# Sixteen sequences of attention and FFN on one core: float copies of three halves of z on ScalarE, and another order of calls ahead of the loop

## Chip, cores and metric

The kernel runs on one core of one Trainium2 chip. The metric is device time in microseconds of one execution; the time before is the median of three runs.

## What is computed

For 16 sequences of 1024 rows of 256 floats, a transformer block with layer norms without weights, in f32:

```python
qkv = einsum('bnd,ed->bne', layernorm(x), W_qkv) + b_qkv      # Q, K, V of 256 each
attn = softmax(Q @ K.T / sqrt(256)) @ V
x = x + layernorm(attn)
h = silu(layernorm(x) @ wg.T) * (layernorm(x) @ wu.T)          # 768 wide, integer weights / 127
x = x + layernorm(h @ wd.T)
```

## The kernel before

Every f32 operand of a product is split into a high and a low f16 part (names ending in h and l), and each product is made of three f16 matmuls (high by high, high by low, low by high; two where the weights are exact in f16). The scores come from one projection: z is x times a matrix A made of Wq and Wk, plus a bias `cb`, and the scores are z times the transposed x. The exponentials times x come next, and the V projection last.

A sequence b has eight tiles of 128 rows, in two groups g of four. For each half of z (b, g), TensorE's `project_z` (`first_z` for b = 0) leaves two PSUM banks. `z_high` on ScalarE (line 502) makes `zTh`, f16, from them; `z_float` on VectorE (line 732) makes the float copy `zw` from the same banks, once its turn in the list has come; `z_low` on GpSimd or VectorE (line 376) subtracts the two into `zTl`. `zw` is one buffer, so a copy waits for the `z_low` ahead of it. `score` of tile i reads `zTh`, `zTl` and the turned x; the banks of z are free for another product when both `zTh` and `zw` are made. Then come `row_max` (VectorE), `exp` and `p_high` (ScalarE), `p_low` (GpSimd; VectorE for tiles 1 and 4), and two transposes by DMA, `turn_p`, issued by SyncE. `Ph` and `Pl` have three slots, so a later `p_high` waits for transposes. `attend` needs the four tiles of its group. Attention's output goes through `o_high`, `o_low` and `project_v` (VectorE's `y_scale`, `y_stats`, GpSimd's `y_norm`), is added to x and normalized (`x1_add`, `x1_norm`, `y_hat`, `y_high`, `y_low`), and turned by `turn_y`. `gate_up` makes two of twelve products a step, `silu`, `h_mul`, `h_high` and `h_low` follow, then `down`.

Weights are scaled and split at run time: `ffn_max` (VectorE) takes the maximum of one matrix, `powers` and `V_scales`, `ffn_scales` make scales of them, `ffn_high` (ScalarE) and `ffn_low` (VectorE) make the f16 parts, `turn_ffn` turns them by DMA.

All order is written out by hand: each of the five engines has one list of such calls, which it works off strictly in that order, each call waiting on semaphores. SyncE's list holds nearly all DMAs. What comes first (sequence 0, and sequence 1's attention scores) is written out call by call; a loop over b = 1 to 12 takes up the rest, in which the feed-forward part of b, the attention of b and the scores of b + 1 are mixed. The change lies in the part written out ahead of that loop; in the loop `z_float` stays on VectorE.

Of the kernel before, what the change touches and what calls it, by code (L numbers as in the profile page):

```python
# [2263 lines left out]
```

## Time and profile before

| | |
|---|---|
| median of 3 runs | 1363.91 us (1363.36 to 1363.94) |
| the profiled execution | 1363.66 us |
| its span in the profile | 1361.9 us |
| TensorE busy | 1347.7 us, 7414 matmuls |
| VectorE, ScalarE, GpSimd busy | 901.8, 878.1, 832.4 us |
| granted TensorE clock | full in all slices |
| mean DMA rate | 115 GB/s |

A profile tells for each engine when each instruction ran and which other engine's signal it had waited for. A matmul's row is longer than the distance to the next one's start, as matmuls overlap, so the busy share says little about small holes; starts in a row say more. The first 105 us are the stretch that the change rewrites, with the first iteration of the loop beginning at 130.

### The profile page before, as it was taken

The numbers are of one execution on the slowest core, as the hardware profiler recorded it, in microseconds if no ns is written. First come the engines' busy times: TensorE is split into PE (matmuls) and PEld (weight loads), VectorE is DVE, ScalarE is ACT, GpSimd is POOL, SyncE is SP. The second block draws the span as 40 slices with busy tenths as digits, with TensorE's granted clock in tenths as the row PEclk, the third lists the DMA queues.
The fourth block names the chain that finished last, engine by engine and source line by source line (L and its number), as shares of the span: only waits on it lengthen the run. The fifth ranks groups of instructions, "written<-read, shape, count | busy, mean of one in ns | idle before, by whom it ended". The sixth has DMA issues, their size and how long they took to land.

```text
span 1361.9 us, 22402 instructions
## 1 busy us (share of the span) xinstructions
PE 1347.7 (99%) x7414; PEld 725.8 (53%) x7414; DVE 901.8 (66%) x2167; ACT 878.1 (64%) x1378; POOL 832.4 (61%) x1001
## 2 busy tenths in 40 slices
PE   8999999999999999999999999999999999999998
PEld 5445455555555555555554555545555555555555
DVE  7895675666766666666766657667666676656556
ACT  6765775666757577475665766567566675756645
POOL 5686483765847648475584746748376584754635
PEclk9999999999999999999999999999999999999999
DMA  5996482835638366392753827448373563725512
GB/s 180 184 194 138 88 153 79 140 101 115 133 86 157 68 132 140 70 169 65 131 132 71 162 79 127 121 92 147 80 142 100 114 134 86 136 66 100 110 32 64
DMA packets 432968, 157.24 MB, mean 115 GB/s; under 512 B 413905, under 2 KB 416337, under 8 KB 432850
## 3 DMA queue, kind: packets, MB, share of 16 engines
q1 hardware_dynamic: 432048, 154.99, 55.2%
q8 instruction: 61, 1.00, 0.3%
q10 hardware_dynamic: 802, 0.79, 0.2%
q14 instruction: 57, 0.47, 0.1%
HBM read 36.70 MB, written 16.78 MB: 39 GB/s over the span
## 4 chain that ended last, share of the span: by engine, by line
PE 92%; POOL 2%; DVE 2%; DMA 2%; ACT 1%; issue 1%; SPq 0%; DVEq 0%; ACTq 0%; POOLq 0%
PE S L868 91%; DMA yTl<-yl 1%; POOL xl L368 1%; POOL Pl L386 0%; POOL yl L413 0%; DVE st L721 0%; DVE S L768 0%; DMA xs<-in_L_attn_t 0%; DVE mxs L739 0%; POOL xs L356 0%; PE S L897 0%; DVE st L777 0%; ACT yn L531 0%; DMA xTl<-xl 0%; POOL rs L331 0%
## 5 line engine op out<-in xcount | busy, mean ns | idle before, releaser
L511 ACT ACTIVATE P<-S,nmx,sc 128x1024 f32<-128x1024 f32 x128 | 153.6, 1200 | 267.1 <-DVE nmx L743 264.9
L805 DVE SCALAR_TENSOR_TENSOR hf<-S,sc,hf 128x512 f32<-128x512 f32 x192 | 141.9, 746 | 140.8 <-ACT hf L546 135.2
L739 DVE TENSOR_REDUCE mxs<-S 128x1 f32<-128x1024 f32 x128 | 156.1, 1220 | 115.7 <-PE S L868 115.7
L386 POOL TENSOR_TENSOR Pl<-P,Ph 128x1024 f16<-128x1024 f32 x96 | 205.1, 2138 | 30.1 <-issue 26.0
L868 PE MATMUL S<-PTh,xh 128*128 128x512 f16 x512 | 194.1, 379 | 0.0
L868 PE MATMUL S<-PTl,xh 128*128 128x512 f16 x512 | 194.0, 379 | 0.0
L868 PE MATMUL S<-PTh,xl 128*128 128x512 f16 x512 | 194.0, 379 | 0.0
L868 PE MATMUL S<-xTh,zTh 128*128 128x512 f16 x506 | 191.8, 379 | 2.0 <-ACT P L511 1.0
L868 PE MATMUL S<-xTh,zTl 128*128 128x512 f16 x508 | 192.5, 379 | 0.0
L868 PE MATMUL S<-xTl,zTh 128*128 128x512 f16 x508 | 192.5, 379 | 0.0
L327 POOL TENSOR_SCALAR rs<-mv,sc 128x2 f32<-128x2 f32 (+2 forms) x96 | 34.6, 361 | 227.4 <-DVE mv L781 184.9
L422 POOL TENSOR_TENSOR hTl<-hf,hTh 128x512 f16<-128x512 f32 x128 | 146.4, 1158 | 42.4 <-ACT hTh L553 42.4
L868 PE MATMUL S<-Wh,hTh 128*128 128x256 f16 x768 | 170.3, 273 | 0.0
L868 PE MATMUL S<-Wh,hTl 128*128 128x256 f16 x768 | 170.3, 273 | 0.0
L546 ACT ACTIVATE hf<-S,sc 128x512 f32<-128x512 f32 x192 | 130.6, 682 | 52.5 <-POOL hTl L422 37.7
L331 POOL TENSOR_TENSOR rs<-rs,mhalf 128x4 f32<-128x4 f32 (+2 forms) x160 | 145.5, 909 | 13.3
L868 PE MATMUL S<-yTh,Gh 128*128 128x512 f16 x384 | 145.6, 379 | 2.4 <-DMA yTl<-yl 2.4
L868 PE MATMUL S<-yTl,Gh 128*128 128x512 f16 x384 | 145.5, 379 | 0.0
L868 PE MATMUL S<-yTh,Uh 128*128 128x512 f16 x384 | 145.5, 379 | 0.0
L868 PE MATMUL S<-yTl,Uh 128*128 128x512 f16 x384 | 145.5, 379 | 0.0
L553 ACT ACTIVATE hTh<-hf 128x512 f16<-128x512 f32 x192 | 119.5, 624 | 35.4 <-DVE hf L805 35.4
L518 ACT ACTIVATE Ph<-P 128x1024 f16<-128x1024 f32 x128 | 134.8, 1054 | 4.2 <-DMA PTl<-Pl 1.1
(155 smaller groups left out, 2486.0 us busy)
## 6 DMA issues: line engine op xcount, KB each, us to landing
xs<-in_L_attn_t SPq DMA_DIRECT2D x32, 512.0 KB, 5.3
X<-in_L_attn_t SPq DMA_DIRECT2D x32, 512.0 KB, 4.5
out_x<-X SPq DMA_DIRECT2D x62, 256.0 KB, 2.9
PTh<-Ph SPq DMA_TRANSPOSE x128, 3.2
PTl<-Pl SPq DMA_TRANSPOSE x128, 3.2
hTl<-in_L_ffn_w_gate SPq DMA_DIRECT2D x1, 768.0 KB, 6.8
hTh<-in_L_ffn_w_up SPq DMA_DIRECT2D x1, 768.0 KB, 8.8
hTl<-in_L_ffn_w_down SPq DMA_DIRECT2D x1, 768.0 KB, 10.1
```

The costliest lines, as they stand in the source:

```text
L327: p.engine.tensor_scalar(rs, var, scalar1=eps, scalar2=mul, op0=ALU.add, **({} if mul is None else {"op1": ALU.mult})).then_inc(g_step, 1)
L331: return p.engine.tensor_tensor(out=rs, in0=rs, in1=mhalf[:, 0:rs.shape[1]], op=ALU.pow)
L368: p.engine.tensor_tensor(out=xl[k][:, gs, :], in0=src, in1=xh[k][:, gs, :], op=ALU.subtract).then_inc(xl_done if b else xl0_done, 1)
L386: p.engine.tensor_tensor(out=Pl[:, m % 3, :], in0=P[:, m % 2, :], in1=Ph[:, m % 3, :], op=ALU.subtract).then_inc(pl_vector if i in PL_ON_V ...
L422: p.engine.tensor_tensor(out=hTl[g][:, c, :], in0=hf[:, n % 3, :], in1=hTh[g][:, c, :], op=ALU.subtract).then_inc(hl_vector if c in HL_ON_ ...
L511: a.engine.activation(P[:, m % 2, :], ps[:, bank:bank + 2, :].rearrange("p a n -> p (a n)"), ACT.Exp, bias=nmx[:, c:c + 1], scale=sS, accu ...
L518: a.engine.activation(Ph[:, m % 3, :], P[:, m % 2, :], ACT.Copy).then_inc(ph_done, 1)
L546: a.engine.activation(hf[:, n % 3, :], ps[:, bank, :], ACT.Silu, scale=sc2[:, 3:4]).then_inc(silu_done, 1)
L553: a.engine.activation(hTh[g][:, c, :], hf[:, n % 3, :], ACT.Copy).then_inc(hh_done, 1)
L739: v.engine.tensor_reduce(mxs[:, c:c + 1], ps[:, bank:bank + 2, :].rearrange("p a n -> p (a n)"), axis=AX.X, op=ALU.max, negate=True).then_ ...
L805: v.engine.scalar_tensor_tensor(out=hf[:, n % 3, :], in0=ps[:, bank + 1, :], scalar=sc2[:, 4:5], in1=hf[:, n % 3, :], op0=ALU.mult, op1=AL ...
L868: done = t.engine.matmul(out, s, m, start=(start and i == 0), stop=(stop and i == len(terms) - 1))
```

## The change

A second function makes the float copy on ScalarE with the same operands, `z_float_scalar`. It takes the place of `z_float` for the halves (0,1), (1,0) and (1,1), standing in ScalarE's list right behind `z_high` of the half (for (1,1) with one `o_high` between). For (0,0), (2,0), (2,1) and in the loop `z_float` stays. In the same stretch the calls of all five lists are put in another order. TensorE's differs in three places, the others' in many. The diff, cut to what the prediction speaks of; a line of "..." marks what is left out:

```diff
+        def z_float_scalar(a, b, g, bank):
+            a.wait_ge(cb_ready, 1)
+            for dj in range(2):
+                a.wait_ge(z_done, 4 * b + 2 * g + dj + 1)
+                zl_wait(a, b if g else b - 1, 1 - g, dj)
+                a.engine.activation(zw[:, dj, :], ps[:, bank + dj, :], ACT.Identity, bias=cb[:, dj:dj + 1], scale=ZS
+                                    ).then_inc(zw_done, 1)
...
@@ SyncE
             turn_p(s, 0, 4, 0)
+            turn_p(s, 0, 4, 1)
             turn_p(s, 0, 5, 0)
             turn_p(s, 0, 5, 1)
-            turn_p(s, 0, 4, 1)
+            turn_ffn(s, 1, 0)
             turn_p(s, 0, 6, 0)
+            turn_p(s, 0, 6, 1)
             turn_v(s, 0)
             turn_v(s, 1)
-            turn_p(s, 0, 6, 1)
             turn_p(s, 0, 7, 0)
...
             turn_p(s, 1, 1, 0)
-            turn_ffn(s, 1, 0)
             reload(s, 0, 0)
             reload(s, 0, 1)
-            turn_p(s, 1, 1, 1)
+            turn_ffn(s, 2, 0)
+            turn_ffn(s, 2, 1)
             turn_ffn(s, 1, 1)
             turn_p(s, 1, 3, 0)
-            turn_ffn(s, 2, 0)
-            turn_ffn(s, 2, 1)
+            turn_p(s, 1, 3, 1)
+            turn_p(s, 1, 1, 1)
             turn_p(s, 1, 2, 0)
             turn_p(s, 1, 2, 1)
             turn_x(s, 2, 0, 0)
             turn_x(s, 2, 0, 1)
-            turn_p(s, 1, 3, 1)
+            turn_p(s, 1, 4, 0)
             turn_y(s, 0, 0, 0)
-            turn_p(s, 1, 4, 0)
             turn_y(s, 0, 0, 1)
...
@@ GpSimd
+            h_low(p, 0, 1, 1)
+            d_norm(p, 0, 0, 0)
+            z_low(p, 2, 1)
             p_low(p, 1, 6)
             p_low(p, 1, 7)
-            z_low(p, 2, 1)
-            h_low(p, 0, 1, 1)
+            x_norm(p, 3, 0)
             d_norm(p, 0, 0, 1)
...
@@ ScalarE
             z_high(a, 0, 1, 2)
+            z_float_scalar(a, 0, 1, 2)
             x_high(a, 1, 0)
             exp(a, 0, 0, 4)
             p_high(a, 0, 0)
             exp(a, 0, 1, 6)
+            p_high(a, 0, 1)
             exp(a, 0, 2, 0)
-            p_high(a, 0, 1)
+            exp(a, 0, 3, 2)
             p_high(a, 0, 2)
+            p_high(a, 0, 3)
             x_high(a, 1, 1)
-            exp(a, 0, 3, 2)
-            p_high(a, 0, 3)
...
             z_high(a, 1, 0, 2)
+            z_float_scalar(a, 1, 0, 2)
+            exp(a, 0, 6, 0)
+            p_high(a, 0, 6)
             V_high(a)
-            exp(a, 0, 6, 0)
+            ffn_high(a, 0)
             o_high(a, 0, 0, 0)
-            p_high(a, 0, 6)
-            ffn_high(a, 0)
+            exp(a, 0, 7, 4)
             ffn_high(a, 1)
-            exp(a, 0, 7, 4)
+            p_high(a, 0, 7)
             exp(a, 1, 0, 0)
-            p_high(a, 0, 7)
-            z_high(a, 1, 1, 0)
             p_high(a, 1, 0)
             ffn_high(a, 2)
+            z_high(a, 1, 1, 0)
             o_high(a, 0, 0, 1)
+            z_float_scalar(a, 1, 1, 0)
             exp(a, 1, 1, 2)
...
@@ VectorE
             V_max(v)
-            z_float(v, 0, 1, 2)
-            row_max(v, 0, 2, 0)
-            z_low(v, 0, 1)
-            row_max(v, 0, 3, 2)
-            p_low(v, 0, 1)
             ffn_max(v, 0)
             ffn_max(v, 1)
+            z_low(v, 0, 1)
+            p_low(v, 0, 1)
+            row_max(v, 0, 2, 0)
+            row_max(v, 0, 3, 2)
             row_max(v, 0, 4, 4)
+            ffn_max(v, 2)
             row_max(v, 0, 5, 6)
-            ffn_max(v, 2)
             row_max(v, 0, 6, 0)
             p_low(v, 0, 4)
+            powers(v, 1, 5, OB[1], ((1, 2, 2.0 ** -100), (2, 5, 1.0)), 1)
+            row_inverse(v, 0, 0)
+            V_scales(v)
             row_max(v, 0, 7, 4)
-            powers(v, 1, 5, OB[1], ((1, 2, 2.0 ** -100), (2, 5, 1.0)), 1)
-            z_float(v, 1, 0, 2)
-            V_scales(v)
             ffn_scales(v)
...
@@ TensorE
+            gate_up(t, 0, 0, 4, 2, (silu_done, 2), (hmul_done, 2), three)
             project_z(t, 2, 1, 6, (silu_done, 3), (hmul_done, 3))
-            gate_up(t, 0, 0, 4, 2, (silu_done, 2), (hmul_done, 2), three)
...
             gate_up(t, 0, 1, 2, 0, (silu_done, 6), (hmul_done, 6), three)
+            down(t, 0, 0, 0, (x1_done, 6), three)
...
-            down(t, 0, 0, 0, (x1_done, 6), three)
...
+            x_first_turn(t, 1, 0)
             first_z(t, 0, 2, 0)
-            x_first_turn(t, 1, 0)
```

## Rows read from the trace of the kernel before

**Rows 1.** The page's head: busy us (share of the span) xinstructions of each engine.

```profile
PE 1347.7 (99%) x7414; PEld 725.8 (53%) x7414; DVE 901.8 (66%) x2167; ACT 878.1 (64%) x1378; POOL 832.4 (61%) x1001
```

**Rows 2.** Timeline of TensorE: start, us, engine line op out<-in xcount [idle before <-releaser].

```profile
27.20 0.38 PE L868 MATMUL S<-xTh,zTl 128*128 128x512 f16 x1
...
27.89 0.39 PE L868 MATMUL S<-xTh,zTh 128*128 128x512 f16 x1 [0.31 <-DVE zw L732]
...
31.36 0.38 PE L868 MATMUL S<-xTh,zTh 128*128 128x512 f16 x1 [0.70 <-issue]
...
39.56 0.39 PE L868 MATMUL S<-xTh,Ah 128*128 128x512 f16 x1 [0.27 <-DMA xTl<-xl]
...
94.64 0.39 PE L868 MATMUL S<-xTh,zTh 128*128 128x512 f16 x1 [1.02 <-ACT P L511]
...
101.44 0.39 PE L868 MATMUL S<-yTh,Gh 128*128 128x512 f16 x1 [1.45 <-DMA yTl<-yl]
...
364.24 0.39 PE L868 MATMUL S<-yTh,Gh 128*128 128x512 f16 x1 [0.39 <-DMA yTl<-yl]
```

**Rows 3.** Chain that ended last, 88 to 101 us: start us, us, what.

```profile
88.48 0.55 DVE S L768 x2
...
94.77 2.10 POOL yl L413
...
96.89 4.51 DMA yTl<-yl
```

**Rows 4.** Instructions of lines 732 and 502: duration ns min/median/max, first and last start.

```profile
L732 DVE TENSOR_SCALAR zw<-S,cb x64: 720/741/752, 17.0 to 1196.2; 128x512 f32<-128x512 f32 x64
...
L502 ACT ACTIVATE zTh<-S,cb x64: 667/680/703, 16.2 to 1195.3; 128x512 f16<-128x512 f32 x64
```

**Rows 5.** Timeline of VectorE, 17 to 37 us.

```profile
17.05 1.40 DVE L732 TENSOR_SCALAR zw<-S,cb 128x512 f32<-128x512 f32 x2
...
23.73 1.23 DVE L739 TENSOR_REDUCE mxs<-S 128x1 f32<-128x1024 f32 x1 [1.89 <-PE S L868]
...
27.10 1.40 DVE L732 TENSOR_SCALAR zw<-S,cb 128x512 f32<-128x512 f32 x2
...
29.79 1.47 DVE L376 TENSOR_TENSOR zTl<-zw,zTh 128x512 f16<-128x512 f32 x2
...
33.69 1.75 DVE L585 TENSOR_REDUCE am<-hTl 128x1 f32<-128x1536 int32 x1
...
35.35 1.74 DVE L585 TENSOR_REDUCE am<-hTh 128x1 f32<-128x1536 int32 x1
```

**Rows 6.** The page's DMA issues: engine op xcount, KB, us to landing.

```profile
hTh<-in_L_ffn_w_up SPq DMA_DIRECT2D x1, 768.0 KB, 8.8
```

**Rows 7.** SyncE's queue in time; then line 276, 30 to 101 us, and its landings.

```profile
14.84 0.55 SPq L300 DMA_DIRECT2D hTh<-in_L_ffn_w_up  x1
...
40.37 2.70 SPq L276 DMA_TRANSPOSE PTl<-Pl  x2
...
55.53 1.31 SPq L276 DMA_TRANSPOSE PTh<-Ph  x1
...
95.19 1.25 SPq L276 DMA_TRANSPOSE PTh<-Ph  x1
...
L276 SPq DMA_TRANSPOSE PTl<-Pl x13: 1231/1325/2394, 30.1 to 98.2; - x13
...
DMA to landing us min/median/max: 3.1/3.3/6.7
```

**Rows 8.** Timelines of ScalarE and GpSimd, 22 to 60 us.

```profile
22.52 1.05 ACT L495 ACTIVATE xh<-xs 128x1024 f16<-128x1024 f32 x1
...
36.27 4.21 POOL L386 TENSOR_TENSOR Pl<-P,Ph 128x1024 f16<-128x1024 f32 x2
...
55.06 1.56 ACT L470 ACTIVATE X<-hTh,sc 128x1536 f16<-128x1536 int32 x1
...
57.71 1.19 ACT L511 ACTIVATE P<-S,nmx,sc 128x1024 f32<-128x1024 f32 x1
```

More of the change, by code:

```diff
@@ L1094, in _ @@
             turn_p(s, 0, 0, 0)
+            turn_p(s, 0, 1, 0)
             turn_p(s, 0, 0, 1)
-            turn_p(s, 0, 1, 0)
             turn_p(s, 0, 1, 1)
             turn_x(s, 1, 0, 1)
+            turn_p(s, 0, 2, 0)
             turn_p(s, 0, 3, 0)
-            turn_p(s, 0, 2, 0)
             turn_p(s, 0, 2, 1)
@@ L1133, in _ @@
             turn_x(s, 2, 0, 1)
-            turn_p(s, 1, 3, 1)
+            turn_p(s, 1, 4, 0)
             turn_y(s, 0, 0, 0)
-            turn_p(s, 1, 4, 0)
             turn_y(s, 0, 0, 1)
-            turn_p(s, 1, 4, 1)
             turn_x(s, 2, 1, 0)
             turn_x(s, 2, 1, 1)
+            turn_p(s, 1, 4, 1)
             load_x(s, 3, 0)
@@ L1145, in _ @@
             turn_y(s, 0, 1, 1)
+            turn_p(s, 1, 5, 1)
             turn_p(s, 1, 6, 0)
-            turn_p(s, 1, 5, 1)
+            turn_p(s, 1, 6, 1)
             turn_p(s, 1, 7, 0)
-            turn_p(s, 1, 6, 1)
             turn_p(s, 1, 7, 1)
@@ L1277, in _ @@
             x_norm(p, 2, 0)
+            x_norm(p, 2, 1)
             p_low(p, 1, 0)
-            x_norm(p, 2, 1)
+            x_hat_pool(p, 2, 1)
             z_low(p, 1, 1)
-            x_hat_pool(p, 2, 1)
             y_norm(p, 0, 0)
@@ L1298, in _ @@
             h_low(p, 0, 1, 0)
+            h_low(p, 0, 1, 1)
+            d_norm(p, 0, 0, 0)
+            z_low(p, 2, 1)
             p_low(p, 1, 6)
             p_low(p, 1, 7)
-            z_low(p, 2, 1)
-            h_low(p, 0, 1, 1)
+            x_norm(p, 3, 0)
             d_norm(p, 0, 0, 1)
-            d_norm(p, 0, 0, 0)
             h_low(p, 0, 1, 3)
+            x_norm(p, 3, 1)
+            p_low(p, 2, 0)
             h_low(p, 0, 1, 4)
-            x_norm(p, 3, 0)
-            p_low(p, 2, 0)
-            x_norm(p, 3, 1)
             for b in range(1, 13):
@@ L1473, in _ @@
             exp(a, 1, 5, 2)
+            p_high(a, 1, 5)
             exp(a, 1, 6, 0)
-            p_high(a, 1, 5)
             z_high(a, 2, 0, 0)
@@ L1484, in _ @@
             h_high(a, 0, 0, 0)
-            p_high(a, 1, 6)
             h_high(a, 0, 0, 1)
+            silu(a, 0, 0, 3, 0)
             h_high(a, 0, 0, 2)
-            silu(a, 0, 0, 3, 0)
+            silu(a, 0, 0, 4, 2)
             z_high(a, 2, 1, 6)
-            silu(a, 0, 0, 4, 2)
-            silu(a, 0, 0, 5, 0)
             h_high(a, 0, 0, 3)
             h_high(a, 0, 0, 4)
-            p_high(a, 1, 7)
+            silu(a, 0, 0, 5, 0)
             silu(a, 0, 1, 0, 2)
@@ L1500, in _ @@
             h_high(a, 0, 1, 1)
+            p_high(a, 1, 6)
+            p_high(a, 1, 7)
             h_high(a, 0, 1, 2)
@@ L1503, in _ @@
             silu(a, 0, 1, 4, 6)
+            silu(a, 0, 1, 5, 0)
+            x_hat(a, 3, 0)
+            o_high(a, 1, 0, 1)
             h_high(a, 0, 1, 3)
-            silu(a, 0, 1, 5, 0)
-            o_high(a, 1, 0, 1)
             h_high(a, 0, 1, 4)
+            exp(a, 2, 0, 0)
             h_high(a, 0, 1, 5)
-            exp(a, 2, 0, 0)
-            x_hat(a, 3, 0)
-            p_high(a, 2, 0)
             o_high(a, 1, 0, 0)
             exp(a, 2, 1, 2)
+            add_bias(a, 0, 0, 1)
+            p_high(a, 2, 0)
             x_hat(a, 3, 1)
-            add_bias(a, 0, 0, 1)
             add_bias(a, 0, 0, 0)
@@ L1777, in _ @@
             row_max(v, 1, 2, 0)
-            ffn_low(v, 1)
             p_low(v, 1, 1)
             y_scale(v, 0, 0, 0)
+            row_inverse(v, 0, 1)
             y_scale(v, 0, 0, 1)
             y_stats(v, 0, 0, 0)
+            ffn_low(v, 1)
             y_stats(v, 0, 0, 1)
@@ L1787, in _ @@
             x1_add(v, 0, 0, 1)
+            o_low(v, 0, 1, 1)
             o_low(v, 0, 1, 0)
-            o_low(v, 0, 1, 1)
             row_max(v, 1, 4, 0)
@@ L1798, in _ @@
             x1_add(v, 0, 1, 0)
+            row_max(v, 1, 7, 2)
             x1_add(v, 0, 1, 1)
-            row_max(v, 1, 7, 2)
             z_float(v, 2, 0, 0)
@@ L1815, in _ @@
             h_mul(v, 0, 1, 2, 0)
+            x_stats(v, 3, 0)
+            x_stats(v, 3, 1)
+            h_low(v, 0, 1, 2)
             h_mul(v, 0, 1, 3, 2)
[L1817 to L1818 removed]
             h_mul(v, 0, 1, 4, 6)
+            d_stats(v, 0, 0, 0)
+            d_stats(v, 0, 0, 1)
             h_mul(v, 0, 1, 5, 0)
[L1821 to L1823 removed]
             d_add(v, 0, 0, 0)
+            d_add(v, 0, 0, 1)
             row_max(v, 2, 0, 0)
             o_low(v, 1, 0, 1)
[L1827 removed]
             h_low(v, 0, 1, 5)
```

35 lines of the change are left out of this document (13 added, 22 removed).

## The prediction

> **What bounds the kernel now.** I read the head of the page first: TensorE is busy 1347.7 of 1361.9 us [rows 1], so a change of order on other engines can only fill or open holes in TensorE's stream. Then TensorE's instructions in order of time. A 512-column matmul starts every 0.216 us, though its row says 0.38, so the idle time in brackets is some 0.16 short of the real hole: after 27.20 the next start was due at 27.42 and came at 27.89, a hole of 0.47 [rows 2]. Read so, the holes of the stretch in front of the loop are, after the first microseconds: 0.47 ahead of 27.89, 0.86 ahead of 31.36, 0.43 ahead of 39.56, 1.18 ahead of 94.64 and 1.61 ahead of 101.44; behind these the timeline has three more up to the end, of about 0.5 each, of which the first is shown, all in front of `gate_up` in the loop, which the change leaves alone [rows 2]. So 4.5 us stand where the change works.
>
> The last view is the chain of waits from 88.5 to 101.4: `project_v` of (0,1) ends, VectorE scales and sums up y, GpSimd makes `yl` at 94.77, its transpose is issued at 96.89 and lands 4.51 later, and only then `gate_up` starts [rows 3]. From Y to `gate_up` are 12.96 us, in which TensorE has four steps of 2.59: 2.6 us of hole whatever comes ahead. The change keeps the order of `y_scale`, `y_stats`, `y_norm` and `y_low` there. So the holes at 94.64 and 101.44 are one hole in two parts and stay; what can be won is 0.47 + 0.86 + 0.43 = 1.76 us.
>
> **Part by part.** I follow each engine's new list with durations and spacings of before, from 14 us to the loop.
>
> *The three float copies.* One copy of half of z is two instructions; on VectorE one takes 741 ns, the ScalarE instruction of the same shape into f16 takes 680 [rows 4]. Float output on ScalarE isn't in the trace for this shape; between 0.55 and 0.75 (either end is near the rows) I take 0.60, since the next instruction starts a little before one's end. For (0,1) ScalarE is through with `zTh` at 22.5, where it went on with x_high [rows 8], and has both halves at 23.8, in place of VectorE's 27.10 to 28.4 [rows 5]. The bank that `score(0,3)` waits for is free long before 27.4: the hole of 0.47 goes. ScalarE's next step, x_high(1,0), ends at 24.8, still ahead of the exp at 25.2, so its 1.2 us are covered there.
>
> The Trainium skill, page "ScalarE: Activation LUTs", section "Rules for kernel authors", speaks against this part: it gives mul and add to VectorE, which per element is up to about 3 times faster in bf16. The trace has ScalarE the faster by 61 ns on this operand out of PSUM, in f32 [rows 4], so the rule doesn't hold here.
>
> *The low part of that half.* `z_low(0,1)` is what ends the hole at 31.36: VectorE ran it from 29.79 to 31.26 [rows 2, 5]. In the new list it stands behind row_max(0,0), row_max(0,1), V_max, and then **ffn_max(0) and ffn_max(1)**, which came later before. VectorE starts row_max(0,0) at 23.8 (23.73, and 0.1 because both `xTl` now come ahead of the copy that began at 17.05, which idle time of VectorE before 17.05 mostly absorbs [rows 5]). V_max ends 3.37 later (23.73 to 27.10), at 27.2; the two maxima cost 1.66 each by their spacing (33.69 to 35.35), to 30.5; z_low takes up to 1.47, to 31.8 or 32.0 [rows 5]. Their data are there: the load of the second matrix is issued at 14.84 and takes 8.8 [rows 6, 7]. TensorE is ready at 30.1 and starts score(0,4) at 31.98 (with 0.1 of signalling, as 31.26 to 31.36), not 31.36. So: 0.1 for the later first copy, less 0.47, plus 0.99 for a hole of 1.85 instead of 0.86: **+0.62** here. Bounds: -0.6 (one maximum hidden by an earlier start) to +0.9.
>
> *The wait at 39.56.* The `xl` behind it comes from GpSimd at 36.3 and lands by 39.3 to 39.5; TensorE arrives at 39.75: the hole of 0.43 goes, net **+0.19**.
>
> *attend(0,0,0) at 45.8.* Behind z_low, VectorE now has p_low(0,1), then row_max(0,2) (33.0) and row_max(0,3) (to 35.8). exp(0,3) follows at 35.8, p_high(0,2) at 37.0 instead of 32: GpSimd, free at 36.1, waits till 38.1 for its two `Pl` of 4.21 together, which ran from 36.27 [rows 8]: done at 42.4 instead of 40.5. SyncE issues the last of them at 42.4 (before, at the end of 40.37 + 2.70), it lands a median 3.3 later, 45.7, and TensorE needs it at 46.0 [rows 7]. Slack 0.3 where it was 0.8: I take 0, bounds 0 and +0.6.
>
> *project_z(1,1) at 59.7.* It waits for exp(1,0), on ScalarE from 57.71 and done at 59.0 [rows 8]. New: V_scales follows TensorE at 49.7, one row_max is put between it and ffn_scales, so ffn_high(0) starts at 53.1, o_high, exp(0,7), ffn_high(1) and p_high(0,7) come behind, exp(1,0) runs 58.7 to 60.0. TensorE is there at 59.9: **+0.2**, bounds 0 and +0.7. The copy for (1,0) ends at 47.9 and the next exp runs before 49.2, needed at 52.1; the one for (1,1) ends at 65.3, its first half at 64.8, and score(1,2) takes them at 65.3 and 66.6. Both cost nothing while ScalarE keeps that lead of some 0.5 us. project_v(0,0) needs o_low at 67.6 and starts at 67.9; o_low(0,1,1) first now waits for ScalarE at 84.3, ends with its partner at 85.7, and project_v(0,1) starts at 86.1: 0.
>
> *SyncE's queue.* Here the order matters most. turn_ffn(1,0) now stands ahead of turn_p(0,6,0) and both turn_v, and waits for ffn_high(1), 1.57 long, begun at 55.06 before and at 56.3 now [rows 8]: it can't be issued before 57.9. SyncE is through with turn_p(0,5,1) at 55.7, idles 2.2 us, and holds eleven and more transposes behind it. Before, it stood at 55.53 with the same set of transposes (only ordered otherwise) up to yTh, and was free at 96.44, 0.45 ahead of yTl [rows 7]. That is a shift of 2.4; 0.6 was idle time before, 0.45 the lead, 0.35 is given by TensorE's own shift, and an emptied queue takes the next transposes at 1.231 instead of 1.325, shortest and median [rows 7]. Left are 0 to 1.0; turn_ffn(2,1), now ahead of five turns of P, waits for ffn_low(2) at 79.3 to 80.3, just when SyncE gets there. I take yTl issued 0.45 late, **+0.45**, bounds 0 and +2.0 (the whole shift arrives). Its 4.51 to landing against a median 3.3 for the `PTl` [rows 3, 7] may be down to what shared the DMA engines then: that could give back up to 1.2.
>
> *From there to the loop.* down(0,0,0) goes ahead of three gate_up and needs `hTl` of chunk 5 at 18.8 us behind the first gate_up; VectorE has it at 18.75: 0, bounds 0 and +0.7. project_z(2,1) and gate_up(0,0,4) swap at no cost, as chunk 3 is ready earlier. x_norm(3,0), x_hat(3,0) and exp(2,0) end about 2 us later than before, relative to TensorE, which had 3 to spare. The loop then starts from the same waits.
>
> **Sum.** 0.1 - 0.47 + 0.99 - 0.43 + 0.2 + 0.45 = +0.84. The profiled execution took 1363.66 us, 1.8 around its span of 1361.9; the median of the three runs is 1363.91, 0.25 above. 1363.91 + 0.8 = **1364.7**. A measurement can tell about 0.2% from no change, 2.7 us.
>
> **Rivals.** (1) Slower: **the stalled queue reaches yTl in full**. Place: turn_ffn(1,0) at 55.7 to 57.9, and again turn_ffn(2,1) at 80. Price: 2.4 less the lead of 0.45 plus 1 us more for ffn_low(2), on top of the +0.4 ahead of it: about +3.3, 1367.2. It decides once yTl is issued later than 99. For it: SyncE issued almost without a break from 55 to 96; against it: the idle 0.6 and the ring's own slack. Chance 0.13. (2) **The maxima don't delay z_low** (VectorE gets ahead, or their order is hidden): the 1.76 go, and yTl lands as quickly as the `PTl`, 1.2 more: up to -2.9, typically -1.8, 1362.1. For it: the copies do leave VectorE; against it: VectorE has no idle time from 23.73 to 31. Chance 0.10, of which 0.03 beyond 0.2%. (3) **The holes only change place**: all is paid back before 101.44 by the fixed 12.96 and the time is 1363.9. Chance 0.15. (4) **ScalarE is slow on float output.** At three times VectorE's 741 ns an instruction takes 2.2 us [rows 4], 3.2 more for a copy; x_high(1,0) and exp(0,0) come about 2 us late, and with them `Pl` and attend(0,0,0): +3, 1366.9. The f16 row of the same shape, 680 ns, speaks against it: 0.02. The factor of three is that of the Trainium skill's page "ScalarE: Activation LUTs", section "Rules for kernel authors".
>
> **How the numbers follow.** The forecast as worked out, +0.2 to +2.5, has 0.60. Faster by over 0.2%: 0.03. Slower by over 0.2%: 0.13 + 0.02, less what of (1) stays under 2.7 us, 0.12. Same: 0.85. The range runs from rival (2) at 1362.3 to rival (1) at 1367.2.
>
> **What would show it.** Right: no hole ahead of score(0,3); one of about 1.9 us ahead of score(0,4), released by VectorE's zTl at 31.9; none at project_z(1,0); SyncE idle at 56 to 58 ahead of the Uh transpose; yTl issued at 97.5 to 98; gate_up from 102 to 102.5. Wrong: row_max(0,0) much earlier than 23.8, a hole in front of an attend (its `Pl` too late), or any new hole between 102 and 131.

## The result, and the profile after

| | before | after |
|---|---|---|
| median, 16 runs each, taken beside one another | 1364.14 us (1363.09 to 1364.78) | 1366.25 us (1364.75 to 1367.42) |
| profiled execution's span | 1361.9 us | 1364.5 us |
| `gate_up` of sequence 0 starts | 101.44 | 103.92 |

The ratio is 1.0015, 95% interval 1.0009 to 1.0022: 2.1 us slower, where +0.8 was forecast. That is inside the range and under 0.2%, but the interval excludes no change. The added time stands ahead of the loop: 2.48 us by the start of `gate_up`. In the loop the two executions differ by little.

Behind line 502 all line numbers are 9 higher than before (868 is 877, 732 is 741, 739 is 748, 681 is 690); `z_float_scalar` is line 511. The head of the page of after, beside [rows 1]:

```profile
span 1364.5 us, 22400 instructions
...
PE 1348.7 (99%) x7414; PEld 726.1 (53%) x7414; DVE 897.1 (66%) x2161; ACT 881.3 (65%) x1384; POOL 829.4 (61%) x1001
```

Six copy instructions (three halves of two banks) have left VectorE and six have come to ScalarE; TensorE's work is the same. Its timeline, beside [rows 2] (start, us, engine line op out<-in, idle time before and releaser):

```profile
17.23 0.38 PE L985 MATMUL S<-xTh,zTh 128*128 128x512 f16 x1 [0.71 <-ACT zTh L502]
19.45 1.04 PE L959 MATMUL S<-xTh,Ah 128*128 128x512 f16 x4 [0.33 <-DVE zw L741]
...
32.48 0.38 PE L877 MATMUL S<-xTh,zTh 128*128 128x512 f16 x1 [1.63 <-issue]
...
61.52 0.39 PE L877 MATMUL S<-xTh,Ah 128*128 128x512 f16 x1 [0.96 <-ACT P L520]
...
87.78 0.27 PE L877 MATMUL S<-Vh,oTh 128*128 128x256 f16 x1 [0.16 <-issue]
...
96.76 0.39 PE L877 MATMUL S<-xTh,zTh 128*128 128x512 f16 x1 [1.02 <-ACT P L520]
...
103.92 0.39 PE L877 MATMUL S<-yTh,Gh 128*128 128x512 f16 x1 [1.80 <-DMA yTl<-yl]
```

As in the prediction, a hole is the start less the due start. The table holds all of them up to `gate_up`; the measured changes add up to the 2.48 us.

| place | hole before | after | change | in the sum |
|---|---|---|---|---|
| start of `first_z(0)` (17.06, 17.23) | – | – | +0.17 | +0.1, with the next line |
| `first_z(1)`, 19.45 | 0 | 0.49 | +0.49 | |
| `score(0,3)`, 27.89 before | 0.47 | 0 | -0.47 | -0.47 |
| `score(0,4)`, 32.48 | 0.86 | 1.80 | +0.94 | +0.99 |
| wait for `xl`, 39.56 before | 0.43 | 0 | -0.43 | -0.43 |
| `project_z(1,1)`, 61.52 | 0 | 1.12 | +1.12 | +0.2 |
| `project_v(0,1)`, 87.78 | 0 | 0.31 | +0.31 | 0 |
| 96.76 and `gate_up`, 103.92 | 1.18, 1.61 | 1.18, 1.96 | +0.35 | +0.45 |

So two terms hold most of the miss, `first_z(1)` and `project_z(1,1)`. I first show what stands behind each in after.

**`first_z(1)`.** VectorE's timeline of after, beside [rows 5]:

```profile
15.21 1.41 DVE L730 BATCH_NORM_STATS2 st<-xs 128x6 f32<-128x256 f32 x4 [0.34 <-DMA xs<-in_L_attn_t]
...
16.82 1.26 DVE L643 SCALAR_TENSOR_TENSOR xTl<-S,xTh 128x512 f16<-128x512 f32 x2
17.99 1.40 DVE L741 TENSOR_SCALAR zw<-S,cb 128x512 f32<-128x512 f32 x2
...
31.09 1.28 DVE L376 TENSOR_TENSOR zTl<-zw,zTh 128x512 f16<-128x512 f32 x2
```

The copy starts at 17.99 and not 17.05. Of the 0.94, about 0.58 are the second `xTl` (1.26 for two, ahead of the copy; before, 0.69 for one) and 0.36 the statistics, which began at 14.85 before and now wait for a load. SyncE issues the feed-forward weights 2 us sooner (the one of `w_up` at 12.83, [rows 7] has it at 14.84), and they take 11.9 us instead of 8.8 [rows 6]; that their earlier issue is what delays the load of x, I only read from this order.

**`project_z(1,1)`.** It waits for `exp(1,0)`, which waits for `ffn_high(0)`, which waits for the scales that VectorE makes. VectorE, then GpSimd, then ScalarE, of after; the last two lines are VectorE and GpSimd of before:

```profile
50.53 1.90 DVE L690 TENSOR_TENSOR sc<-sc 128x1 f32<-128x1 f32 x1
...
48.05 2.28 POOL L376 TENSOR_TENSOR zTl<-zw,zTh 128x512 f16<-128x512 f32 x2 [3.06 <-ACT zw L511]
50.29 4.21 POOL L386 TENSOR_TENSOR Pl<-P,Ph 128x1024 f16<-128x1024 f32 x2
...
54.63 1.57 ACT L470 ACTIVATE X<-hTl,sc 128x1536 f16<-128x1536 int32 x1 [3.24 <-DVE sc L591]
...
60.18 1.19 ACT L520 ACTIVATE P<-S,nmx,sc 128x1024 f32<-128x1024 f32 x1
...
49.85 0.92 DVE L681 TENSOR_TENSOR sc<-sc 128x1 f32<-128x1 f32 x1
...
48.48 2.28 POOL L376 TENSOR_TENSOR zTl<-zw,zTh 128x512 f16<-128x512 f32 x2 [5.92 <-DVE zw L732]
```

The squaring of one number in each partition takes 1.90 us. It took 0.92 before, and that was no fair price either: it ends at 52.43, GpSimd's first `Pl` at 50.29 + 4.21 / 2 = 52.40; before it ended at 50.77, GpSimd's `zTl` at 50.76. `exp(1,0)` comes at 60.18 where I had 58.7.

**SyncE.** The queue of after, beside [rows 7], then VectorE, then GpSimd:

```profile
54.80 1.34 SPq L276 DMA_TRANSPOSE PTl<-Pl  x1
59.36 1.44 SPq L311 DMA_TRANSPOSE Uh<-X  x1
...
96.73 1.27 SPq L276 DMA_TRANSPOSE PTh<-Ph  x1
98.04 1.32 SPq L282 DMA_TRANSPOSE yTh<-yh  x1
99.41 1.43 SPq L282 DMA_TRANSPOSE yTl<-yl  x1
...
83.10 0.88 DVE L799 SCALAR_TENSOR_TENSOR X<-S,rs,X 128x256 f32<-128x256 f32 x2 [2.12 <-DMA X<-in_L_attn_t]
...
96.85 2.14 POOL L413 TENSOR_TENSOR yl<-yn,yh 128x1024 f16<-128x1024 f32 x1
```

SyncE idles from 56.14 to 59.36 for `turn_ffn(1,0)`. The reload of x that stands behind it comes late, VectorE waits 2.12 us for it at 83.10, and `project_v(0,1)` starts 0.31 late. `yl` is done at 98.99, and its transpose is issued at 99.41, as SyncE is still with `yTh`: the 0.45 of the prediction.

### The profile page after: what moved, and what is told of

Its sections match the earlier page's. It is cut to its first block, busy times and chain, and to the rows that moved or that the text cites. A ratio compares the mean times of both kernels' runs of the same rounds, so it can differ in the third digit from the quotient of the medians.

```text
span 1364.5 us, 22400 instructions
## 1 busy us (share of the span) xinstructions
PE 1348.7 (99%) x7414; PEld 726.1 (53%) x7414; DVE 897.1 (66%) x2161; ACT 881.3 (65%) x1384; POOL 829.4 (61%) x1001
## 4 chain that ended last, share of the span: by engine, by line
PE 87%; SPq 3%; DVE 3%; DMA 2%; issue 2%; ACT 2%; POOL 1%; DVEq 0%; ACTq 0%; POOLq 0%
PE S L877 87%; SPq L276 2%; DMA yTl<-yl 1%; SPq L257 1%; DVE mxs L748 1%; ACT Ph L527 1%; DVE S L777 1%; DVE st L786 0%; POOL Pl L386 0%; DMA PTl<-Pl 0%; SPq L282 0%; DMA xs<-in_L_attn_t 0%; ACT P L520 0%; SPq L246 0%; PE S L906 0%
## 6 DMA issues: line engine op xcount, KB each, us to landing
hTh<-in_L_ffn_w_up SPq DMA_DIRECT2D x1, 768.0 KB, 11.9
```

## The experiments

Every kernel below computes the whole result. Times are medians. Each group of kernels ran on a chip of its own with the kernel before in between (its medians there: 1363.88 to 1364.01, and 1364.14 beside after), and the ratio is to those runs; so medians of different rows compare to some 0.3 us at best. "Start" is the start of `gate_up` in the profile; the median less this start lies between 1261.8 and 1263.4 for all kernels, with 1262.7 before and 1262.3 after, so the start tells what the stretch ahead of the loop does, and under 1 us is lost or won behind it. A start is that of one profiled execution; one kernel that was profiled twice (copies_only) started at 102.85 and at 103.31, so a difference of under 0.5 us between starts is not shown by itself.

| kernel | median us (runs) | ratio, 95% interval | start |
|---|---|---|---|
| before | 1364.14 (16) | 1 | 101.44 |
| after | 1366.25 (16) | 1.0015 (1.0009 to 1.0022) | 103.92 |
| copies_only | 1366.27 (11) | 1.0016 (1.0007 to 1.0025) | 102.85 |
| order_only | 1369.60 (5) | 1.0041 (1.0027 to 1.0055) | 107.61 |
| zlow_first | 1369.62 (5) | 1.0041 (1.0027 to 1.0055) | 106.46 |
| zlow_quiet | 1367.54 (8) | 1.0027 (1.0016 to 1.0037) | 104.62 |
| square_scalar | 1365.03 (11) | 1.0005 (0.9996 to 1.0014) | 102.03 |
| uh_late | 1365.48 (11) | 1.0008 (0.9999 to 1.0017) | 103.64 |
| head_before | 1366.02 (11) | 1.0016 (1.0007 to 1.0025) | 103.29 |
| three | 1364.69 (11) | 1.0006 (0.9997 to 1.0015) | 101.91 |
| all_four | 1368.06 (9) | 1.0026 (1.0016 to 1.0036) | 104.95 |
| three_quiet | 1366.13 (11) | 1.0016 (1.0007 to 1.0025) | 103.39 |
| tuned | 1363.39 (11) | 0.9996 (0.9987 to 1.0005) | 100.49 |

### copies_only and copies_again: the copies without the new order

```diff
@@ ScalarE's list of before, behind z_high of each half
+            z_float_scalar(a, 0, 1, 2)
+            z_float_scalar(a, 1, 0, 2)
+            z_float_scalar(a, 1, 1, 0)
@@ VectorE's list of before
-            z_float(v, 0, 1, 2)
-            z_float(v, 1, 0, 2)
-            z_float(v, 1, 1, 0)
```

> The kernel before with the three float copies on ScalarE, each right behind z_high of its half, and no other change of order. Theory (the 2.1 us come from the new order, not from the copies): the hole ahead of score(0,3) (0.47) goes and the one ahead of score(0,4) falls from 0.86 to 0.3, but xTl of x(1,0) still lands at 39.5, so the hole at project_z(1,0) grows from 0.43 to about 1.5 and TensorE leaves it where it did before; the time is within 0.3 us of before. Rival (ScalarE's 3.6 us of added work are what costs: its exps come later): exp(0,0) or exp(1,0) late, a hole at project_z(1,1) or an attend, and 1 to 2 us slower than before.

Measured: +2.3 us in the median, as much as the whole change; +1.41 us by the start of `gate_up` (after: +2.48). TensorE, then VectorE, then GpSimd, of copies_only:

```profile
31.30 0.38 PE L877 MATMUL S<-xTh,zTh 128*128 128x512 f16 x1 [1.19 <-issue]
...
49.14 0.38 PE L944 MATMUL S<-pw,one 1*128 1x8 f32 x2 [0.63 <-DVE pw L663]
...
68.88 0.27 PE L877 MATMUL S<-Vh,oTh 128*128 128x256 f16 x1 [0.58 <-DVE oTl L765]
...
28.95 2.25 DVE L376 TENSOR_TENSOR zTl<-zw,zTh 128x512 f16<-128x512 f32 x2
...
46.98 0.79 DVE L656 TENSOR_SCALAR ax<-ax 1x1 f32<-1x1 f32 x2
47.80 1.08 DVE L660 TENSOR_SCALAR pw<-ax 1x4 int32<-1x4 int32 x1
...
27.92 2.13 POOL L386 TENSOR_TENSOR Pl<-P,Ph 128x1024 f16<-128x1024 f32 x1
...
46.59 2.27 POOL L376 TENSOR_TENSOR zTl<-zw,zTh 128x512 f16<-128x512 f32 x2 [4.09 <-ACT zw L511]
```

The hole ahead of `score(0,3)` goes, but `z_low(0,1)` starts 0.84 sooner, while GpSimd's `Pl` still runs, and takes 2.25 instead of 1.47: `score(0,4)` starts at 31.30, as before. At 47 the copy for (1,0) comes sooner too, GpSimd's `z_low(1,0)` starts at 46.59 instead of 48.48, and VectorE's three little `powers` steps, 0.22 for the first two and 0.16 for the third in before, take 0.79 and 1.08 beside it: a new hole of 0.79 at 49.14. The hole of 0.74 at 68.88 is a late `oTh`: ScalarE starts it at 67.30 instead of 65.52, of which the copy for (1,1) is some 1.1 and a later z the rest. That is the recorded rival, ScalarE's added work, and it holds for this one hole. The holes changed place and grew. The theory, that this kernel would stand where before stands, fell.

Since the loop's holes of this profile (0.41, 1.32, 0.75, 0.44) were larger than those of others, the same kernel was profiled once more:

> The same kernel as copies_only once more, for its profile alone. If its loop's holes (3.0 us together in its first profile, 1.5 in those of before and of the changed kernel) belong to its order, they come back, each at the same place and size; if they come from the moment at which the DMA engines were held up in one execution, their sum changes by 0.5 us or more while gate_up starts at 102.8 again.

Measured: 1365.74 in one run. Ahead of the loop the same holes again (1.33, 0.44, 0.99, 0.73, 1.17, 1.69), `gate_up` at 103.31; in the loop 0.27, 0.76, 0.28 and 0.13. So what stands ahead of the loop repeats within 0.2 us a hole, and the loop's holes vary from execution to execution by some 1.5 us together. I read nothing from single holes in the loop.

### order_only: the new order without the copies

```diff
@@ after: the three z_float_scalar leave ScalarE's list; in VectorE's:
             V_max(v)
+            z_float(v, 0, 1, 2)
             ffn_max(v, 0)
...
+            z_float(v, 1, 0, 2)
...
+            z_float(v, 1, 1, 0)
```

> The changed kernel's new order with the three float copies left on VectorE: (0,1) behind V_max, (1,0) behind powers, (1,1) behind o_low(0,0,0). Theory (the copies on ScalarE help inside the new order where VectorE is packed, at (0,1), by their 1.3 us): the two maxima and z_low(0,1) come 1.3 us later, score(0,4) starts at 33.8 instead of 32.48, and as the holes of 61.52 and gate_up depend on what follows TensorE, the kernel is 1 to 2 us slower than the changed one, 3 to 4 slower than before. Rival (ScalarE's 3.6 us more cost what VectorE wins): equal to the changed kernel within 0.4 us.

Measured: +5.6 us against before, 3.4 more than after, where 1 to 2 more were expected. TensorE, then VectorE, then GpSimd, of order_only:

```profile
35.85 0.38 PE L877 MATMUL S<-xTh,zTh 128*128 128x512 f16 x1 [4.57 <-issue]
...
37.25 0.63 PE L877 MATMUL S<-xTh,zTl 128*128 128x512 f16 x1
37.68 0.63 PE L877 MATMUL S<-xTh,zTh 128*128 128x512 f16 x1
...
32.36 3.39 DVE L376 TENSOR_TENSOR zTl<-zw,zTh 128x512 f16<-128x512 f32 x2
...
32.65 2.55 POOL L368 TENSOR_TENSOR xl<-xs,xh 128x1024 f16<-128x1024 f32 x1
```

With the copy on VectorE, `z_low(0,1)` starts at 32.36 instead of 31.09, and there its second instruction meets GpSimd's `xl`: 3.39 us for the two and a hole of 4.72. The 0.47 ahead of `score(0,3)` is there again as before (28.52), the wait for `xl` isn't. The matmuls behind the long hole start 0.43 apart and not 0.216; the last section has more on that. At 55.59 the squaring takes only 0.50, and `project_z(1,1)` has no hole. The two parts of the change don't add up (copies alone +2.3, order alone +5.6, both +2.1): each moves the time at which `z_low` meets GpSimd, and together they happen to miss it. That after stands no worse than copies_only is luck of this meeting, and nothing in the prediction foresaw it.

### zlow_first and zlow_quiet: the two maxima, and GpSimd beside z_low

```diff
@@ zlow_first: VectorE's list of after
             V_max(v)
+            z_low(v, 0, 1)
             ffn_max(v, 0)
             ffn_max(v, 1)
-            z_low(v, 0, 1)
@@ zlow_quiet: this, and in GpSimd's list
-            p_low(p, 0, 0)
             x_hat_pool(p, 1, 1)
+            p_low(p, 0, 0)
```

> The changed kernel with z_low(0,1) on VectorE ahead of ffn_max(0) and ffn_max(1), nothing else. By the prediction's term (0.99 for the longer hole) the 1.80 us ahead of score(0,4) go and the kernel is 1 to 1.8 us faster than the changed one. Rival: xTl of x(1,0), issued at 36.96 and landed at 40.2, is the next bound 0.1 us behind; the hole moves to project_z(1,0) nearly whole (1.5 to 1.8 us there), and the gain is 0.1 to 0.3 us.

> The changed kernel with z_low(0,1) ahead of the two ffn_max, as in zlow_first, and on GpSimd x_hat_pool(1,1) ahead of p_low(0,0), so that GpSimd runs instructions with one tensor operand where it ran the subtraction. Theory (VectorE's z_low, two SBUF operands, took 3.68 us in zlow_first because GpSimd's subtraction of xl and Pl ran beside it): z_low takes 1.3 to 1.9 us, the holes of 0.87 at score(0,4) and 2.70 at score(0,6) shrink to under 0.6 each, gate_up starts 3 us or more before that of zlow_first (106.46). Rival (z_low is slow for another reason, its place behind V_max): still 3 us and more, time as zlow_first, 1369.6.

Measured: zlow_first loses another 3.4 us against after, zlow_quiet 1.3; neither came out as expected. VectorE, GpSimd, TensorE of zlow_first, then VectorE of zlow_quiet:

```profile
27.39 3.68 DVE L376 TENSOR_TENSOR zTl<-zw,zTh 128x512 f16<-128x512 f32 x2
...
28.06 2.46 POOL L386 TENSOR_TENSOR Pl<-P,Ph 128x1024 f16<-128x1024 f32 x1
...
39.05 0.39 PE L877 MATMUL S<-xTh,zTh 128*128 128x512 f16 x1 [2.54 <-ACT P L520]
...
27.57 1.73 DVE L376 TENSOR_TENSOR zTl<-zw,zTh 128x512 f16<-128x512 f32 x2
```

`z_low` takes 3.68 us instead of 1.28, `score(0,4)` starts 1.3 sooner (31.17, a hole of 0.87, as before), and the row maxima behind the two `ffn_max` come later: 2.70 of hole at `score(0,6)`, 0.80 at 45.04 and some 0.7 at the first `attend`. In zlow_quiet GpSimd runs the four short `x_hat` steps where `Pl` stood: `z_low` takes 1.73, the hole at `score(0,4)` is gone, 1.53 of hole stay at 37.20 and 0.79 at 43.19 (and 0.6 at the first `attend`). So the neighbour on GpSimd sets the duration of `z_low`: that is shown. And the maxima take the same 3.3 us of VectorE wherever they stand ahead of `row_max(0,2)` and `row_max(0,3)`: with `z_low` quick, zlow_quiet is still slower than after.

### square_scalar: the squaring in another form

```diff
-            v.engine.tensor_tensor(out=eps2, in0=eps2, in1=eps2, op=ALU.mult).then_inc(eps2_ready, 1)
+            v.engine.tensor_scalar(eps2, eps2, scalar1=eps2, scalar2=None, op0=ALU.mult).then_inc(eps2_ready, 1)
```

> The changed kernel with the squaring of eps2 in V_scales (a 128x1 instruction with two SBUF operands that took 1.90 us) written as a product with a per-partition scalar, one tensor operand. Theory (that instruction waits for GpSimd's two Pl subtractions, and exp(1,0) and the Uh transpose hang on it): it takes some 0.15 us, ffn_high(0) starts 1.7 us earlier, the hole of 1.12 at project_z(1,1) goes, Uh is issued 1.7 us earlier and the holes of 0.31 and 0.35 behind it shrink: 1.1 to 1.7 us faster than the changed kernel, which would be 0.4 to 1 slower than before. Rival (a 128x1 instruction is slow there whatever its operands): still over 1 us, and no gain.

Measured: 1.2 us under after in the median (the two intervals against before overlap; the profile carries the reading). VectorE, then GpSimd, then ScalarE, of square_scalar:

```profile
50.48 0.21 DVE L690 TENSOR_SCALAR sc<-sc 128x1 f32<-128x1 f32 x1
...
50.23 4.22 POOL L386 TENSOR_TENSOR Pl<-P,Ph 128x1024 f16<-128x1024 f32 x2
...
58.44 1.20 ACT L520 ACTIVATE P<-S,nmx,sc 128x1024 f32<-128x1024 f32 x1
```

The same product at the same place beside the same two `Pl`: 0.21 us instead of 1.90. `exp(1,0)` comes 1.74 sooner, and the hole of 1.12 at `project_z(1,1)`, that of 0.31 and 0.38 of the last one are gone: `gate_up` at 102.03, 1.9 sooner. This settles the largest missing term. It is one line, and no part of the change: the change only moved the line under a longer GpSimd instruction.

### uh_late and head_before: SyncE's order, and the first 19 us

```diff
@@ uh_late: SyncE's list
-            turn_ffn(s, 1, 0)
...
             turn_p(s, 1, 1, 0)
+            turn_ffn(s, 1, 0)
@@ head_before: ScalarE's list
-            x_first_scalar(a, 6, 7)
+            A_high(a)
...
-            A_high(a)
+            x_first_scalar(a, 6, 7)
```

In head_before VectorE's and TensorE's lists are put in before's order up to 19 us as well.

> The changed kernel with turn_ffn(1,0), the Uh transpose, back behind turn_p(1,1,0) in SyncE's list as before. Theory (SyncE's idle time from 56.1 to 59.4 pushes all transposes up to yTl): no idle time there, reload of X and the yTl transpose 2 us or more earlier, VectorE's 2.1 us of waiting for X and the hole of 0.31 at project_v(0,1) go, the 1.96 ahead of gate_up falls to 1.6: 0.6 us faster than the changed kernel. The hole at project_z(1,1) stays. Rival (the queue's delay is covered): under 0.2 us.

> The changed kernel with the order of before in its first 19 us on ScalarE, VectorE and TensorE (A_high ahead of the transposed x, tiles 6 and 7 behind it, first_z ahead of x_first_turn). Theory (tiles 6 and 7 done earlier let SyncE issue the 2.3 MB of weights 2 us earlier, against which the load of x(1,0) runs until 15.2, so VectorE's statistics and the first float copy are late): the loads of weights start at 14.4 again, the first float copy at 17.1 instead of 18.0, the hole of 0.49 ahead of first_z(1) goes, and 0.3 to 0.6 us are won. Rival (the next wait, z_low behind the maxima, is set by other things): no gain.

Measured: uh_late 0.8 under after, head_before 0.2 under it, neither told apart from it by its interval; against its own runs of before head_before is at 1.0016, as after at 1.0015, so its times show no gain. In uh_late SyncE issues without a break from 50.1 to 69.4, the reload of x is in time, the hole of 0.31 is gone, and the 1.10 at `project_z(1,1)` stays: the idle queue is not behind that one. (The 0.31 is gone in square_scalar and head_before as well, where VectorE still waits 1.70 and 1.88 for the reload.) But `gate_up` starts only 0.28 sooner. GpSimd and SyncE of uh_late:

```profile
96.53 2.13 POOL L413 TENSOR_TENSOR yl<-yn,yh 128x1024 f16<-128x1024 f32 x1
...
98.69 1.23 SPq L282 DMA_TRANSPOSE yTl<-yl  x1
```

SyncE is free and issues `yTl` as soon as `yl` is there, 0.03 behind it where it was 0.42 in after, and the transpose then takes 4.90 to land instead of 4.46. What makes one landing 4.46 and another 4.90 was not tried. In head_before the hole at `first_z(1)` is gone and `gate_up` starts at 103.29, 0.63 sooner; the loop of that execution had more holes, and the median shows next to nothing of it. The hole is shown to come from the order of the first 19 us; which part of it is the second `xTl` and which the load was only read, not separated.

### three, all_four, three_quiet: the repairs together

> The changed kernel with the squaring on one tensor operand, Uh late and the head as before; z_low stays behind the maxima. If the three effects add up (gate_up 1.9, 0.3 and 0.6 us earlier than 103.92) it starts at 101.1 to 101.5, as before's 101.44, and the time equals before within 0.7 us. If one of them only covers another: gate_up at 102 or later, 1 us slower than before.

> The changed kernel with all four: z_low(0,1) first, the squaring with one tensor operand, Uh late, the head as before. If the single effects add up: 0.5 + 0.1 to 0.9 + 1.1 to 1.7 + 0.6, so 2.3 to 3.7 us faster than the changed kernel, at or up to 1.5 us below before. If xTl of x(1,0) holds TensorE at 40 as before: equal to before within 0.3 us.

> The three edits of the run before together with z_low(0,1) first and GpSimd's two calls swapped. If z_low is quick, TensorE gets to project_z(1,0) at or before the landing of xTl at 39.5, and gate_up starts at 100.5 to 101.3: 0.2 to 0.9 us faster than before. If GpSimd's later Pl(0,0) holds exp(0,2) and score(0,6): 0 to 1 us slower than before.

three is after with square_scalar, uh_late and head_before; all_four adds zlow_first, three_quiet zlow_quiet. three has one hole left ahead of 95, 1.88 at 32.25, and its `gate_up` at 101.91 is no more than 0.12 sooner than square_scalar's alone. The three gains (1.9, 0.3, 0.6) don't add. Each of the three kernels by itself already lacks the 0.31 at `project_v(0,1)`, so their sum counts it three times, 0.6 us of the 0.8 that are missing. And against square_scalar three is rid of the 0.60 ahead of `first_z(1)`, but its `first_z(0)` starts 0.34 later (17.42, 17.08) and its hole ahead of `score(0,4)` is 0.09 longer. all_four and three_quiet lose 3.4 and 1.4 us against three in the median, by the same holes as zlow_first and zlow_quiet; the gains expected of them did not come.

### tuned: z_low where GpSimd is soonest through, and the maxima last

```diff
@@ three, and VectorE's list
             V_max(v)
-            ffn_max(v, 0)
-            ffn_max(v, 1)
             z_low(v, 0, 1)
-            p_low(v, 0, 1)
             row_max(v, 0, 2, 0)
             row_max(v, 0, 3, 2)
+            p_low(v, 0, 1)
             row_max(v, 0, 4, 4)
+            ffn_max(v, 0)
+            row_max(v, 0, 5, 6)
+            ffn_max(v, 1)
             ffn_max(v, 2)
-            row_max(v, 0, 5, 6)
```

GpSimd's list there is x_low(0,0), x_low(1,0), x_hat_pool(1,1), p_low(0,0), x_low(0,1), and SyncE's has turn_x(1,0,1) behind turn_p(0,0,0).

> As run three (squaring on one tensor operand, Uh late, head as before), and: VectorE does z_low(0,1), row_max(0,2), row_max(0,3) and p_low(0,1) ahead of all three ffn_max; GpSimd does x_low(1,0) second and x_hat_pool(1,1) third, ahead of p_low(0,0) and x_low(0,1); SyncE issues turn_x(1,0,1) behind turn_p(0,0,0). Theory: z_low on VectorE runs beside GpSimd's one-operand instructions and is done by 29.0, no hole ahead of score(0,4), score(0,6) and project_z(1,0); attend(0,0,0) starts at 44.2 to 44.8 (before: 45.81), and gate_up at 99.9 to 100.7 (before: 101.44): 0.7 to 1.5 us faster than before. Rival (the gain is taken back by a wait for Pl or its transpose at score(0,7) or attend(0,0,0)): gate_up at 101 to 102, as before.

Measured: 2.9 us under after, and the intervals of the two against before lie apart (up to 1.0005, from 1.0009). TensorE, then VectorE, then GpSimd, of tuned:

```profile
17.27 0.38 PE L985 MATMUL S<-xTh,zTh 128*128 128x512 f16 x1 [0.74 <-ACT zTh L502]
...
44.86 0.38 PE L877 MATMUL S<-PTh,xh 128*128 128x512 f16 x1 [0.48 <-DMA PTl<-Pl]
...
100.49 0.39 PE L877 MATMUL S<-yTh,Gh 128*128 128x512 f16 x1 [1.46 <-DMA yTl<-yl]
...
27.30 2.07 DVE L376 TENSOR_TENSOR zTl<-zw,zTh 128x512 f16<-128x512 f32 x2
...
32.05 2.45 DVE L386 TENSOR_TENSOR Pl<-P,Ph 128x1024 f16<-128x1024 f32 x1
...
26.10 2.12 POOL L368 TENSOR_TENSOR xl<-xs,xh 128x1024 f16<-128x1024 f32 x1
...
33.38 3.11 POOL L368 TENSOR_TENSOR xl<-X,xh 128x1024 f16<-128x1024 f32 x1
```

Between 17.27 and the hole at 93.67 one new hole is left, of some 0.6 (0.48 and the 0.16 of overlap) at the first `attend`, whose `Pl` comes late. The 1.76 us that the prediction named as all there is to win are won, less this 0.6 and 0.21 of a later start: `gate_up` at 100.49 is 0.95 sooner than before. By the start, then, the forecast held. The median is 0.6 under before's, interval 0.9987 to 1.0005: it can't be told from before, and the 0.7 to 1.5 us that were expected are not shown. How much of this order before could use with the copies left on VectorE was not tried.

## Why the prediction was right, and where it wasn't

**Right in sign and within its range, for reasons of which half held.** The steps that held: the copy on ScalarE is quick (line 511 takes 0.695 a piece, 0.57 from start to start, 0.60 was taken), so the rival of a slow ScalarE is out; the hole ahead of `score(0,3)` goes; that ahead of `score(0,4)` becomes 1.80 (1.85 forecast) with `z_low` at 31.09 to 32.37; the wait at 39.56 goes; `attend(0,0,0)` isn't delayed; `yTl` is issued 0.40 behind its place (0.45 forecast) and the y part costs +0.35; nothing new from 104 to 131. Rival (1), the stalled queue in full, didn't come: SyncE idled 3.2 us and caught up, and of the 2.5 us lost uh_late gives 0.3 back by its profile. The sign that was named for it, `yTl` issued later than 99, did come (99.41), but says nothing: it was a time from the start, and `yl` itself was there only at 98.99. Rival (3), holes that only change place and cost nothing, failed for after, and in copies_only the holes changed place but grew.

That +2.1 fell between +0.2 and +2.5 is in part luck. The upper part of that band was there for SyncE's queue (its bound was +2.0, and it cost 0.35), while by the profile the missing 1.64 us come from three other terms: +0.92 at `project_z(1,1)`, beyond its own bound, +0.56 at the first copy and +0.31 at `project_v(0,1)`, which was put at 0 (less 0.15 elsewhere). `gate_up` was to start from 102 to 102.5 and started at 103.92. Rival (2) is also given two times, 1362.1 and, as the lower end of the range, 1362.3; nothing hangs on it.

**The term that was mis-sized: `project_z(1,1)`, +0.2 with an upper bound of +0.7, and 1.12 measured.** I took the durations of VectorE's scale chain over from before as if they were prices of the work. The 0.92 for a squaring of 128 numbers, beside about 0.15 for each of its one-column neighbours (lines 582 and 709 of before), was the sign that it held a wait, and a moved instruction meets another one. The traces show the rule of that wait. Each row gives when VectorE's instruction ended, when the GpSimd instruction that ran at its start (or had slipped in between the pair) ended, and what is left:

| VectorE | starts, us | ends | GpSimd's ends | left | its length when undisturbed |
|---|---|---|---|---|---|
| before, squaring | 49.85, 0.92 | 50.77 | `zTl` 50.76 | 0.01 | 0.16 (line 718) |
| before, a product in `ffn_scales` (706) | 51.85, 1.01 | 52.86 | `Pl` 52.85 | 0.01 | 0.16 |
| after, squaring | 50.53, 1.90 | 52.43 | `Pl` 52.40 | 0.03 | 0.16 |
| copies_only, squaring | 50.49, 0.47 | 50.96 | `Pl` 50.95 | 0.01 | 0.16 |
| square_scalar, a product in `ffn_scales` (715) | 53.13, 1.33 | 54.46 | `Pl` 54.45 | 0.01 | 0.16 |
| after, `ffn_low` (722) | 60.63, 3.53 | 64.16 | `Pl` 62.54 | 1.62 | 1.81 |
| copies_only, `z_low` x2 | 28.95, 2.25 | 31.20 | `Pl` 30.05 | 1.15 | 1.28 |
| zlow_first, `z_low`, the second | 28.45, 2.62 | 31.07 | `Pl` 30.52 | 0.55 | 0.64 |
| order_only, `z_low`, the second | 32.36, 3.39 for both | 35.75 | `xl` 35.20 | 0.55 | 0.64 |
| tuned, `z_low` x2 | 27.30, 2.07 | 29.37 | `xl` 28.22 | 1.15 | 1.28 |
| tuned, `p_low` | 32.05, 2.45 | 34.50 | `Pl` 33.42 | 1.08 | 1.22 |

What is left is the instruction's own length, less 0.1 to 0.2 in each row: VectorE's instruction doesn't run slowly beside GpSimd, it stands still until GpSimd's ends and then takes its own time. It goes the other way round as well: in tuned, `xl` is on GpSimd's engine from 33.38, VectorE's `p_low` ends at 34.50, and 1.99 later, about its own 2.12, `xl` ends. The Trainium skill states this as a lock on a shared pair of SBUF ports (page "SBUF — State Buffer", section "Who interferes with whom"): a VectorE instruction with two SBUF inputs and a GpSimd instruction that reads SBUF exclude each other for their whole length, whichever starts first. The trace agrees, by the table. Weighed ahead of the prediction, it would have given the hole: the squaring, 0.7 us later than before, meets the first of two `Pl`, on GpSimd from 50.3, and must wait for its end at 52.4.

The same rule bears on the maxima ahead of `z_low`. Their term was right in size: +0.99 booked, +0.94 measured. What it didn't say is that moving `z_low` alone ahead of them wins nothing. Behind them it starts at 31.09, past the end of `Pl` at 30.57, in the stretch in which GpSimd runs `x_hat`, four instructions of 0.54 each, of which it need wait for one at most. Ahead of them (zlow_first) it starts at 27.39 and takes 3.68, and the maxima still stand ahead of the row maxima that `score(0,6)` waits for, which cost 2.70 there. Only tuned, with the maxima behind `row_max(0,2)` and `row_max(0,3)` as well, has neither hole.

**Second: the first copy, +0.1 forecast, 0.49 and 0.17 measured.** I wrote that idle time before 17.05 mostly absorbs the second `xTl`. In before that idle time (0.74 us) lies at 12.61, ahead of statistics that must come first, and in after only 0.30 of it is left at 12.55 and a wait of 0.34 for a load stands right ahead of the statistics. Of a step that is moved I had followed the instruction and not the loads that now came sooner. The 0.17 is within what `first_z(0)` varies from kernel to kernel (16.94 to 17.69).

**Third: SyncE's idle time at 56, booked only as a delay of `yTl`.** Its other customer was the reload of x, 25 us later: 0.31 at `project_v(0,1)`, taken away by uh_late (and by square_scalar and head_before).

**What stays open.** The profile gives +2.48 at `gate_up` and the medians +2.1; the rest lies in the loop, whose holes vary too much for one profile to say. Why the transpose of `yl` takes 4.5 to 4.9 to land where the median of `PTl` over the whole run is 3.2 wasn't tried.

## What to carry to other kernels

Before moving an instruction, look at what its duration in the trace consists of: one that costs several times its neighbours of the same shape may hold a wait (those looked at here did), and at its new place it will hold another. For each VectorE instruction with two inputs in SBUF, find the GpSimd instruction beside it, at the old and the new place, and add the time to its end; for a one-column instruction that waits, a form with a per-partition scalar may be free of it. Where a change shifts the order of several engines, don't add up its parts as measured alone: here they were +2.3 and +5.6 and the whole +2.1.
